# One early constant block instead of two layers' worth, group statistics in three groups, and the convolutional layers in a new order

## The chip, the core and the metric

The kernel runs on one NeuronCore of a Trainium2 chip. Such a core has five engines that run side by side: TensorE (PE) does matrix products and writes them to PSUM banks, VectorE (DVE) does elementwise work and reductions, ScalarE (ACT) does activations and copies, GpSimd (POOL) does elementwise work on SBUF, and SyncE (SP) issues transfers. Each engine works through its own list of instructions in order, and an instruction waits where it needs a semaphore that another engine, or a transfer, raises. The metric is the device time of one execution in microseconds (us), taken as the median of several runs.

## The reference, cut to what matters

The input is `x`, four images of 128 channels and 16 x 16 pixels. It goes through two convolutional layers (the first is an attention over the pixels of each image), then two attention layers with a small network each, on 256 tokens per image. The change touches the first two.

```python
def L0(x):                                  # attention over the pixels
    h = group_norm(x, gamma, beta)          # 32 groups of 4 channels, eps 1e-6
    q, k, v = (conv1x1(h, w, b) for w, b in ((wq, bq), (wk, bk), (wv, bv)))
    a = softmax(q.T @ k / sqrt(C))          # 256 x 256 for each image
    return x + conv1x1(v @ a.T, wp, bp)
def L1(x):                                  # squeeze and expand
    h = normalize_groups(x)                 # eps 1e-5
    s = relu(conv1x1(h, squeeze_w, squeeze_b))
    return x + concat(relu(conv1x1(s, expand1x1)), relu(conv3x3(s, expand3x3)))
# then: sliding-window attention, quantized linear layer, causal attention,
# and a mixture of 8 experts (2 per token), each behind a layer norm
```

## The kernel before, in words

Everything is in SBUF for the whole run. An image n (0 to 3) is one tile of 128 channels x 256 pixels: `xs` is the input, `hn` the normed image, `x1` the sum after the first layer (the trace writes `x`), `conv_out` the second layer's product, `t` the tokens (pixels on the partitions), `ht` the normed tokens and `hT` these turned back. `bank` are the 8 PSUM banks; an image has two of them in the convolutional layers (`two`), and an image of a pair has four of its own in the attention layers (`lane`). Images 0 and 1 are the pair that goes through the attention layer first, images 2 and 3 follow half a layer behind.

The order of the work is written out by hand: each engine's block is a long list of calls such as `first_project(1)` or `largest(0, 1, 2)`, one list for an engine, and only semaphores tie the lists together. No scheduler is at work.

The constants are one packed matrix of 4160 columns, `pk`. ACT loads the first 136 columns (`group`, `vecs`), SP loads the columns from `FIRST` to `EARLY` (semaphore `consts_in`) and from `EARLY` to the end (`consts2_in`), then the experts' weights.

Stages, with the names that the steps below use:

- Group statistics. DVE takes mean and variance of each channel (`first_stats`, `group_moments`), PE averages them over the four channels of a group with a product with `group` (`group_stats`), DVE makes a variance (`group_variance`), POOL raises it to -1/2 (L417, `grstd`), and DVE applies it (`affine` and `normed_input` in the first layer, `normed_residual` in the second). It is done for two pairs of images, `PAIRS`.
- First layer: `fold` multiplies wv by wp once, `first_project` makes q and k, `first_values` the values, `first_scores` the scores, DVE their maxima (`first_largest`) and ACT the exponentials (`first_exps`), DVE divides (`first_probs`), PE turns them (`first_turn`) and mixes the values (`first_mix`), DVE adds the input (`first_residual`, L1595).
- Second layer: `squeeze`, ACT and DVE copy it into a padded image (`squeezed`), `convolve`, ACT `convolved`, DVE `second_residual` (L1624).
- Tokens: `turn_tokens` on PE, `tokens` on DVE, `norm_variance` on DVE, POOL `power` (L381), DVE `norm` (L1437), PE `turn`, ACT `turned`.
- Entry of attention: PE `project_keys` (L889) and `project_queries` (L900), ACT `upper_keys` and `upper_queries`, DVE `lower_keys` (L1445) and `lower_queries` (L1451), PE `values`, DVE `copy_values`, `masked_keys` on DVE, ACT and POOL, PE `scores`, DVE `largest` (L1475), ACT `exps`, PE `turn_probs` (L955), and DVE or ACT copy them back.

`keep_clock` issues matmuls on a zeroed tile `idle_work` whose results nobody reads. POOL waits in `after_norm(0, 3)` for DVE's `norm(0, 3)`, then makes the quantized weight (L442 to L451) and splits the experts' weights into two parts (L432, L434), between which its parts of `masked_keys` and `power` for the next images stand.

Of the kernel before, what the change touches and what calls it, by code (L numbers as in the profile page):

```python
# [14 lines left out]
B, HH, WW = 4, 16, 16  # L15
# [34 lines left out]
EARLY = AT["aq"]  # L50
# [4 lines left out]
def build(nc, x, packed, w1, w2, routes, out):  # L55
    with ExitStack() as ctx:
# [312 lines left out]
        def _(pool):  # L369
# [43 lines left out]
            for j in range(2):  # L413
                for p, ns in enumerate(PAIRS):
                    pool.wait_ge(ve_ready, 2 * j + p + 1)
# [42 lines left out]
            power(0, 2)  # L458
            power(0, 3)
            masked_keys(0, 0)  # L460
# [74 lines left out]
        def _(act):  # L535
# [125 lines left out]
            first_exps(0)  # L661
            first_queries(2)
            first_keys(2)
            first_queries(3)
            first_keys(3)
            first_exps(1)
            first_exps(2)
            first_probs_turned(0)
# [4 lines left out]
            squeezed(0)  # L673
            squeezed(1)
            convolved(0)
            convolved(1)
            squeezed(2)
            squeezed(3)
            convolved(2)
            convolved(3)  # L680
            turned(0, 0)
            turned(0, 1)
            upper_keys(0, 0)
            upper_queries(0, 0)
# [3 lines left out]
            masked_keys(0, 1, 1)  # L688
            exps(0, 1, 0)
            exps(0, 0, 0)  # L690
# [87 lines left out]
            upper_keys(1, 2)  # L778
            masked_keys(1, 3, 0)
            upper_queries(1, 2)  # L780
            inverse_sums_turned(1, 1)
# [16 lines left out]
            exps(1, 2, 3)  # L798
            exps(1, 3, 4)
            exps(1, 2, 4)  # L800
            probs_turned(1, 3, 3)
            probs_turned(1, 2, 3)
            exps(1, 3, 5)
            exps(1, 2, 5)
            exp_of_gap(0)
            probs_turned(1, 3, 5)
            probs_turned(1, 2, 5)
            turn_routes(0)
            inverse_sums_turned(1, 3)
            inverse_sums_turned(1, 2)  # L810
# [30 lines left out]
        def _(pe):  # L841
            mm = nc.tensor.matmul

            def group_stats(j, p):
                pe.wait_ge(cs_ready, 2 * j + p + 1)
                ns = PAIRS[p]
                mm(two[ns[0]][1][:, 0:4], const("group"), cmv[:, ns[0]:ns[-1] + 1, :],
                   start=True, stop=True).then_inc(gs_ready, 1)
# [254 lines left out]
            def squeeze(n):  # L1103
                pe.wait_ge(hn_ready, B + n + 1)
# [873 lines left out]
```

## Time and profile before

| | us |
|---|---|
| median of 3 runs | 238.69 (238.41 to 238.84) |
| the profiled execution | 238.59 |
| its span, first to last instruction | 236.8 |
| PE busy | 225.3 |
| DVE busy | 204.7 |
| ACT busy | 168.1 |
| POOL busy | 92.1 |

The profiled execution is 1.79 us longer than its span, and 0.10 us shorter than the median. The two convolutional layers take the first 37 us, the two attention layers run to about 143 us, and the experts take the rest. The share of busy time does not say what bounds a stage; the waits in it do.

### The profile page before, as it was taken

What the parts mean: (1) busy time and instruction counts of PE and PEld (TensorE: products, weight loads), DVE (VectorE), ACT (ScalarE), POOL (GpSimd) and SP (SyncE); (2) the same over time, 40 slices, a digit from 0 to 9 for tenths busy, and PEclk for the clock granted to TensorE, in tenths of its full rate; (3) what the DMA queues carried; (4) which work ended last, traced back from release to release, by engine and by line L of the source; (5) the groups of instructions that cost most, each with busy time, mean ns of one, the idle gap of its engine ahead of it and who ended that gap; (6) DMA issues with size and microseconds to landing.
All of it is one profiled execution on the core that took longest, in us unless ns stands there. A gap on an engine that the chain in (4) does not pass through costs nothing.

```text
span 236.8 us, 4624 instructions
## 1 busy us (share of the span) xinstructions
PE 225.3 (95%) x1495; PEld 172.5 (73%) x1495; DVE 204.7 (86%) x524; ACT 168.1 (71%) x498; POOL 92.1 (39%) x155
## 2 busy tenths in 40 slices
PE   7899898999999999999999998999999999999995
PEld 2697566677776687676876675887888888888885
DVE  4678889985989989999798965999999996799986
ACT  2276355899769997799969968666557766666660
POOL 6200325668885856277825819924200000000000
PEclk9999999999999999999999999999999999999999
DMA  6910000000310300030000303510110002612001
GB/s 177 373 45 4 0 0 0 1 3 14 121 47 4 89 0 3 0 93 0 3 1 0 91 1 116 155 44 28 55 53 0 3 0 79 190 44 79 13 1 44
DMA packets 9463, 11.71 MB, mean 49 GB/s; under 512 B 720, under 2 KB 6096, under 8 KB 9312
## 3 DMA queue, kind: packets, MB, share of 16 engines
q1 hardware_dynamic: 9008, 11.16, 15.3%
q10 hardware_dynamic: 432, 0.27, 0.4%
q8 instruction: 12, 0.20, 0.3%
q14 instruction: 11, 0.09, 0.1%
HBM read 10.87 MB, written 0.56 MB: 48 GB/s over the span
## 4 chain that ended last, share of the span: by engine, by line
PE 61%; DVE 14%; ACT 9%; POOL 9%; DMA 3%; issue 3%; SPq 1%; POOLq 0%; ACTq 0%; DVEq 0%
PE bank L1031 6%; PE bank L1046 6%; PE bank L1043 6%; PE bank L1044 6%; PE bank L1033 6%; PE bank L1032 6%; ACT early_prob L588 4%; PE bank L955 4%; DVE negmax L1475 4%; POOL w_lo L434 3%; DMA pk<-packed 3%; PE bank L980 2%; PE bank L889 2%; PE bank L931 2%; POOL w_hi L432 2%
## 5 line engine op out<-in xcount | busy, mean ns | idle before, releaser
L821 ACT ACTIVATE hb<-bank,pk 128x512 f32<-128x512 f32 x64 | 43.0, 710 | 19.6 <-PE bank L1033 19.6
L1853 DVE TENSOR_TENSOR hlo<-hb,hhi 128x512 fp32r<-128x512 f32 x64 | 46.1, 741 | 4.8 <-ACT hhi L824 3.7
L588 ACT ACTIVATE prob<-bank,negmax 128x192 f32<-128x192 f32 (+1 forms) x64 | 28.8, 480 | 5.5 <-DVE negmax L1475 5.2
L1475 DVE TENSOR_REDUCE negmax<-bank 128x2 f32<-128x384 f32 (+2 forms) x48 | 29.8, 640 | 2.7 <-PE bank L937 2.3
L544 ACT ACTIVATE probT<-bank 128x512 f32<-128x512 f32 x38 | 23.0, 639 | 5.9 <-PE bank L955 4.3
L1031 PE MATMUL bank<-xhi,w_hi 128*128 128x512 f32 x64 | 25.6, 399 | 1.2 <-ACT hhi L824 1.1
L434 POOL TENSOR_TENSOR w_lo<-w_raw,w_hi 128x256 fp32r<-128x256 f32 x32 | 25.2, 788 | 2.6
L1043 PE MATMUL bank<-hhi,w_hi 128*128 128x512 f32 (+2 forms) x68 | 25.9, 381 | 0.0
L1046 PE MATMUL bank<-hlo,w_hi 128*128 128x512 f32 (+2 forms) x68 | 25.9, 381 | 0.0
L1044 PE MATMUL bank<-hhi,w_lo 128*128 128x512 f32 (+2 forms) x68 | 25.8, 380 | 0.0
L1033 PE MATMUL bank<-xhi,w_lo 128*128 128x512 f32 x64 | 25.0, 390 | 0.0
L1032 PE MATMUL bank<-xlo,w_hi 128*128 128x512 f32 x64 | 25.0, 390 | 0.0
L931 PE MATMUL bank<-kM,q_hi 128*128 128x512 f32 (+1 forms) x48 | 22.6, 471 | 1.6 <-ACT early_prob L588 1.0
L588 ACT ACTIVATE early_prob<-bank,negmax 128x128 f32<-128x128 f32 x64 | 23.3, 416 | 0.3 <-DVE negmax L1475 0.2
L824 ACT ACTIVATE hhi<-bank,pk 128x512 fp32r<-128x512 f32 x32 | 22.6, 707 | 0.0
L381 POOL TENSOR_TENSOR rstd<-ve,neghalf 128x2 f32<-128x2 f32 x16 | 11.6, 733 | 25.7 <-DVE ve L1432 25.7
L955 PE MATMUL bank<-pk,prob 128*128 128x128 f32 x128 | 19.4, 276 | 0.6 <-ACT prob L588 0.6
L432 POOL CAST w_hi<-w_raw 128x256 fp32r<-128x256 f32 x32 | 14.5, 453 | 11.2 <-DVE comb L1510 5.3
L409 POOL TENSOR_SCALAR kM<-k_parts,pk 128x256 fp32r<-128x256 f32 x32 | 17.4, 569 | 2.4 <-DVE k_parts L1445 2.3
L931 PE MATMUL bank<-kM,q_lo 128*128 128x512 f32 (+1 forms) x48 | 18.1, 376 | 0.0
L955 PEld LDWEIGHTS bank<-pk,prob 128*128 128x128 f32 x128 | 14.8, 141 | 3.2 <-issue 1.2
L588 ACT ACTIVATION_READ_ACCUMULATOR early_prob<-bank,negmax 128x1 f32 x64 | 16.4, 256 | 0.0
(159 smaller groups left out, 525.2 us busy)
## 6 DMA issues: line engine op xcount, KB each, us to landing
w_raw<-w SPq DMA_DIRECT2D x16, 256.0 KB, 3.1
comb_b<-routes SPq DMA_DIRECT2D x16, 256.0 KB, 3.2
pk<-packed SPq DMA_DIRECT2D x1, 1280.0 KB, 8.9
pk<-packed SPq DMA_DIRECT2D x1, 560.0 KB, 6.3
xs<-x SPq DMA_DIRECT2D x3, 128.0 KB, 2.6
out<-acc SPq DMA_DIRECT2D x3, 128.0 KB, 1.7
xs<-x ACTq DMA_DIRECT2D x1, 128.0 KB, 3.0
pk<-packed ACTq DMA_DIRECT2D x1, 68.0 KB, 2.5
```

Source lines behind the costliest of these rows:

```text
L588: last = nc.scalar.activation(prob_of(n, u)[:, of], lane[n][u % 2][:, of], ACT.Exp, bias=negmax[n][:, unit_query(u), h:h + 1], accum_out=s ...
L821: nc.scalar.activation(hb[blk % 2][:, j, :], h_bank[j][:, :], ACT.Relu, bias=bias).then_inc(h_ready, 1)
L931: mm(dst[:, :, keys], part[n % 2][:, g, i * 128:(i + 1) * 128], kM[n % 2][:, heads[0]:heads[-1] + 1, keys], start=(part is q_hi), stop=Fal ...
L955: last = nc.tensor.transpose(lane[n][2][:, i * 128:(i + 1) * 128], prob_of(n, u)[:, i * 128:(i + 1) * 128], ident)
L1031: mm(h_bank[j][:, :], w_hi[e][:, 0, chunk], xhi[:, cols], start=True, stop=False)
L1032: mm(h_bank[j][:, :], w_hi[e][:, 0, chunk], xlo[:, cols], start=False, stop=False)
L1033: mm(h_bank[j][:, :], w_lo[e][:, 0, chunk], xhi[:, cols], start=False, stop=True).then_inc(h_full, 1)
L1043: mm(sums, w_hi[e][:, 1, chunk], hhi[blk % 2][:, j, cols], start=(j == 0), stop=False)
L1044: mm(sums, w_lo[e][:, 1, chunk], hhi[blk % 2][:, j, cols], start=False, stop=False)
L1046: last = mm(sums, w_hi[e][:, 1, chunk], hlo[blk % 2][:, j, cols], start=False, stop=(j == HC - 1))
L1475: V.tensor_reduce(negmax[n][:, unit_query(u), heads[0]:heads[-1] + 1], lane[n][u % 2][:, :].rearrange("q (h k) -> q h k", h=len(heads))[:, ...
L1853: V.tensor_tensor(hlo[blk % 2][:, j, :], hb[blk % 2][:, j, :], hhi[blk % 2][:, j, :].bitcast(F32), ALU.subtract).then_inc(hlo_ready, 1)
```

## The change

Four things are changed. The early constant block ends before `squeeze` instead of before `aq` (640 columns instead of 1120), SP issues the third image behind it, and waits for it to land before it issues the other constants; `squeeze(0)` waits for these. Group statistics are made for images 0, 1 and the pair (2, 3) instead of two pairs, in both layers. The fixed lists of PE, DVE, ACT and POOL are written in a new order, mostly in the convolutional layers and at the entry of attention, with a few neighbours exchanged further on. The idle matmuls go from 8, 5, 1, 6 and 1 in a row to 8, 3, 3, 3, 1 and 1.

```diff
-EARLY = AT["aq"]
+EARLY = AT["squeeze"]
+GROUPS = (((0,), (1,), (2, 3)), ((0,), (1,), (2, 3)))
+def group_of(j, p):
+    return j * len(GROUPS[0]) + p
...
         def _(sp):
-            for n in range(B - 1):
+            for n in range(B - 2):
                 sp.dma_start(xs[n][:, :], x[n]).then_inc(x_in[n], 16)
             sp.dma_start(pk[:, FIRST:EARLY], packed[:, FIRST:EARLY]).then_inc(consts_in, 16)
+            sp.dma_start(xs[B - 2][:, :], x[B - 2]).then_inc(x_in[B - 2], 16)
+            sp.wait_ge(consts_in, 16)
             sp.dma_start(pk[:, EARLY:PACKED], packed[:, EARLY:PACKED]).then_inc(consts2_in, 16)
...
             def group_stats(j, p):
-                pe.wait_ge(cs_ready, 2 * j + p + 1)
-                ns = PAIRS[p]
-                mm(two[ns[0]][1][:, 0:4], const("group"), cmv[:, ns[0]:ns[-1] + 1, :],
+                pe.wait_ge(cs_ready, group_of(j, p) + 1)
+                if (j, p) == (1, 0):
+                    pe.wait_ge(w_mean_read, 1)
+                ns = GROUPS[j][p]
+                mm(two[ns[0]][j][:, 0:2 * len(ns)], const("group"), cmv[:, ns[0]:ns[-1] + 1, :],
...
             def first_values(n):
                 pe.wait_ge(fold_ready, 1)
+                pe.wait_ge(hn_ready, n + 1)
...
             def squeeze(n):
+                if n == 0:
+                    pe.wait_ge(consts2_in, 16)
...
             def group_moments(j, p):
-                ns = PAIRS[p]
+                ns = GROUPS[j][p]
...
             second_residual(2)
-            norm(0, 0)
+            norm(0, 1)
             second_residual(3)
-            norm(0, 1)
+            lower_queries(0, 0)
             tokens([2, 3])
-            norm_variance([2, 3])
+            norm_variance([2])
             lower_keys(0, 0)
-            lower_queries(0, 0)
             lower_keys(0, 1)
+            norm_variance([3])
```

The first instructions of DVE, from the first image's statistics to the variance of the first group; `cmv` holds each image's moments, `gve` the variance. Before:

```order
L1395 BN_STATS stats0<-xs0 128x6
L1395 BN_STATS stats1<-xs1 128x6
L1403 BN_AGGR cmv<-stats0 128x2
L1403 BN_AGGR cmv<-stats1 128x2
L1406 TENSOR_TENSOR csq<-cmv 128x2
L1407 TENSOR_TENSOR cmv<-cmv,csq 128x2
```

And in the changed kernel:

```order
L1414 BN_STATS stats0<-xs0 128x6
L1422 BN_AGGR cmv<-stats0 128x2
L1425 TENSOR_TENSOR csq<-cmv 128x1
L1426 TENSOR_TENSOR cmv<-cmv,csq 128x1
L1414 BN_STATS stats1<-xs1 128x6
L1422 BN_AGGR cmv<-stats1 128x2
```

The pair's steps on two columns have become one image's steps on one column, and the second image's own follow.

DVE again, where the second layer ends and attention begins: `x13` is image 3 after the second layer, `q_lo0` and `k_parts0` are the first lane's queries and keys. Before:

```order
L1624 TENSOR_TENSOR x13<-x13,conv_out3 128x256
L1437 TENSOR_SCALAR ht1<-t1,mv1,rstd1 128x128 x2
L1629 COPY t2<-bank3 128x256
L1629 COPY t3<-bank7 128x256
L1423 BN_STATS stats2<-t2 128x6 x2
L1423 BN_STATS stats3<-t3 128x6 x2
L1428 BN_AGGR mv2<-stats2 128x2 x2
L1428 BN_AGGR mv3<-stats3 128x2 x2
L1432 TENSOR_SCALAR ve2<-mv2 128x2
L1432 TENSOR_SCALAR ve3<-mv3 128x2
L1445 TENSOR_TENSOR k_parts0<-bank1,k_parts0 64x512
```

And in the changed kernel:

```order
L1456 TENSOR_SCALAR ht1<-t1,mv1,rstd1 128x128 x2
L1644 TENSOR_TENSOR x13<-x13,conv_out3 128x256
L1470 SCALAR_TENSOR_TENSOR q_lo0<-bank0,q_hi0 128x512
L1649 COPY t2<-bank3 128x256
L1649 COPY t3<-bank7 128x256
L1442 BN_STATS stats2<-t2 128x6 x2
L1447 BN_AGGR mv2<-stats2 128x2 x2
L1451 TENSOR_SCALAR ve2<-mv2 128x2
L1464 TENSOR_TENSOR k_parts0<-bank1,k_parts0 64x512
L1464 TENSOR_TENSOR k_parts1<-bank5,k_parts1 64x512
L1442 BN_STATS stats3<-t3 128x6 x2
```

`ht1` now stands ahead of `x13`, and `q_lo0`, which stood behind all of these rows, now follows `x13` directly.

PE at the same place, where `x13` is turned into tokens (bank7) and the first lane's projections follow. Before:

```order
L1099 MATMUL bank3<-pk,x12 128x128 x2
L862 MATMUL bank0<-pk,ht0 128x128 x2
L1099 MATMUL bank7<-pk,x13 128x128 x2
L862 MATMUL bank4<-pk,ht1 128x128 x2
L889 MATMUL bank1<-hT0,pk 128x256 x2
```

And in the changed kernel:

```order
L875 MATMUL bank0<-pk,ht0 128x128 x2
L1127 MATMUL bank2<-spad2,pk 128x256 x3
L1127 MATMUL bank6<-spad3,pk 128x256 x3
L1113 MATMUL bank3<-pk,x12 128x128 x2
L875 MATMUL bank4<-pk,ht1 128x128 x2
L1113 MATMUL bank7<-pk,x13 128x128 x2
L913 MATMUL bank0<-hT0,pk 128x256 x2
L902 MATMUL bank1<-hT0,pk 128x256 x2
```

The first lane's `ht0` is turned before the last two convolutions, the turn of `x13` is now the last matmul ahead of the projections, and the queries (L913) come before the keys (L902).

## Rows read from the trace of the kernel before

**Rows 1.** Windows: start:end, length, busy us (count) per engine, granted clock, DMA share, GB/s

```profile
core 0: us, PE busy (x) PEld busy (x) DVE busy (x) ACT busy (x) POOL busy (x), PEclk, DMA share, GB/s
0.00:12.00 12.00, 9.55 (x38) 5.49 (x39) 6.59 (x32) 3.42 (x8) 5.10 (x15) 1.00 0.82 276
...
28.00:37.00 9.00, 7.82 (x38) 5.71 (x36) 7.21 (x27) 4.57 (x11) 3.30 (x7) 1.00 0.00 0
37.00:50.00 13.00, 12.35 (x78) 8.88 (x77) 12.59 (x34) 10.19 (x40) 6.71 (x12) 1.00 0.00 1
50.00:66.00 16.00, 16.00 (x166) 12.44 (x165) 12.10 (x23) 14.55 (x54) 14.28 (x25) 1.00 0.19 61
```

**Rows 2.** Transfers of the page: count, KB each, median us from issue to landing

```profile
pk<-packed SPq DMA_DIRECT2D x1, 1280.0 KB, 8.9
pk<-packed SPq DMA_DIRECT2D x1, 560.0 KB, 6.3
```

**Rows 3.** Timeline, 0 to 12 us: start, us, engine, line, operation [idle before, releaser]

```profile
1.17 3.60 PE L1053 MATMUL bank<-idle_work 128*128 128x512 bf16 x8 [1.17 <-DVE idle_work L1633]
...
5.43 1.33 PE L1053 MATMUL bank<-idle_work 128*128 128x512 bf16 x5
...
6.39 0.70 POOL L417 TENSOR_TENSOR grstd<-gve,neghalf 128x2 f32<-128x2 f32 x1 [2.26 <-DVE gve L1415]
...
8.04 0.73 DVE L1573 TENSOR_SCALAR hn<-xs,ga,gb 128x256 f32<-128x256 f32 x2
...
8.41 0.49 PE L1093 MATMUL bank<-pk 128*128 128x128 f32 x2 [0.95 <-DMA pk<-packed]
...
8.88 0.68 PE L1057 MATMUL bank<-hn,pk 128*128 128x256 f32 x2
```

**Rows 4.** Windows of DVE alone: start:end, length, busy us (count), granted clock, DMA

```profile
11.78:36.52 24.74, 20.42 (x71) 1.00 0.04 13
19.98:28.26 8.28, 7.63 (x30) 1.00 0.01 2
36.52:49.14 12.62, 12.21 (x34) 1.00 0.00 1
```

**Rows 5.** DVE groups by line, 0 to 37 us: busy us, mean ns, idle before

```profile
L1573 DVE TENSOR_SCALAR hn<-xs,ga,gb 128x256 f32<-128x256 f32 x4 | 1.5, 406 | 0.0
L1406 DVE TENSOR_TENSOR csq<-cmv 128x2 f32<-128x2 f32 x4 | 0.6, 161 | 0.1
L1565 DVE TENSOR_TENSOR ga<-grstd,pk 128x1 f32<-128x1 f32 x4 | 0.5, 156 | 0.6 <-POOL grstd L417 0.6
```

**Rows 6.** Waits of DVE, 11.7 to 36.5 us: total us, times, longest

```profile
DVE negmax L1582 <- PE bank L1070: 1.7, 2, 1.3
DVE hn L1600 <- POOL grstd L417: 0.8, 1, 0.8
DVE rinv L1587 <- ACT prob L626: 0.7, 1, 0.7
DVE ht L1437 <- POOL rstd L381: 0.6, 1, 0.6
```

**Rows 7.** Timeline, 36 to 39.3 us, of DVE, then PE, then ACT

```profile
36.10 0.42 DVE L1624 TENSOR_TENSOR x<-x,conv_out 128x256 f32<-128x256 f32 x1
36.43 0.60 DVE L1437 TENSOR_SCALAR ht<-t,mv,rstd 128x128 f32<-128x128 f32 x2
36.95 0.75 DVE L1629 COPY t<-bank 128x256 f32<-128x256 f32 x2
...
39.19 0.69 DVE L1445 TENSOR_TENSOR k_parts<-bank,k_parts 64x512 fp32r<-64x512 f32 x1
...
36.57 0.44 PE L1099 MATMUL bank<-pk,x 128*128 128x128 f32 x2
...
37.36 1.03 PE L889 MATMUL bank<-hT,pk 128*128 128x256 f32 x4
...
38.43 0.60 ACT L544 ACTIVATE k_parts<-bank 128x512 fp32r<-128x512 f32 x1 [0.48 <-PE bank L889]
```

**Rows 8.** Timeline, 48.5 to 71 us, of DVE and POOL around POOL's long row of work

```profile
48.54 0.59 DVE L1437 TENSOR_SCALAR ht<-t,mv,rstd 128x128 f32<-128x128 f32 x2
...
49.23 0.73 POOL L442 TENSOR_SCALAR w_less<-pk,w_mean 128x128 f32<-128x128 f32 x1 [4.18 <-DVE ht L1437]
...
68.83 0.18 DVE L1432 TENSOR_SCALAR ve<-mv 128x2 f32<-128x2 f32 x1
...
69.79 0.73 POOL L381 TENSOR_TENSOR rstd<-ve,neghalf 128x2 f32<-128x2 f32 x1
...
70.56 0.60 DVE L1437 TENSOR_SCALAR ht<-t,mv,rstd 128x128 f32<-128x128 f32 x2 [0.50 <-POOL rstd L381]
```

More of the change, by code:

```diff
@@ L1174, in _ @@
             values(0, 1)
+            scores(0, 0, 0)
             scores(0, 1, 0)
-            scores(0, 0, 0)
             scores(0, 1, 1)
+            turn_probs(0, 0, 0)
             scores(0, 0, 1)
+            scores(0, 0, 2)
             turn_probs(0, 1, 0)
             scores(0, 1, 2)
-            turn_probs(0, 0, 0)
-            scores(0, 0, 2)
+            turn(0, 2)
             scores(0, 1, 3)
-            turn(0, 2)
             mix(0, PAIRS[0], 0)
@@ L1221, in _ @@
             turn_probs(0, 3, 0)
+            scores(0, 2, 2)
+            turn_probs(0, 2, 0)
             scores(0, 3, 2)
-            turn_probs(0, 2, 0)
-            scores(0, 2, 2)
             turn(1, 1)
@@ L1645, in _ @@
+            affine(1)
+            group_moments(0, 2)
             normed_input(1)
-            affine(1)
+            first_values(0)
+            group_variance(0, 2, 1e-6)
+            affine(2)
+            first_largest(0)
             normed_input(2)
             normed_input(3)
-            first_values(0)
-            first_largest(0)
+            first_largest(1)
+            first_probs(0)
             weight_sums()
-            first_probs(0)
-            first_largest(1)
+            first_probs(1)
@@ L1677, in _ @@
-            squeezed(0)
+            group_moments(1, 2)
+            second_residual(0)
             squeezed(1)
-            group_variance(1, 1, 1e-5)
+            group_variance(1, 2, 1e-5)
+            tokens([0])
+            norm_variance([0])
             normed_residual(2)
             normed_residual(3)
-            second_residual(0)
+            second_residual(1)
+            norm(0, 0)
             squeezed(2)
-            second_residual(1)
+            tokens([1])
             squeezed(3)
-            tokens([0, 1])
@@ L1698, in _ @@
             lower_queries(0, 1)
-            masked_keys(0, 0, 0)
+            largest(0, 0, 0)
             copy_values(0, 1)
+            masked_keys(0, 0, 1)
             largest(0, 1, 0)
-            masked_keys(0, 0, 1)
-            largest(0, 0, 0)
             largest(0, 1, 1)
+            copy_probs(0, 0, 0)
             largest(0, 0, 1)
+            norm(0, 2)
             copy_probs(0, 1, 0)
-            norm(0, 2)
-            copy_probs(0, 0, 0)
+            norm(0, 3)
             largest(0, 0, 2)
-            norm(0, 3)
@@ L1825, in _ @@
             norm(3, 0)
+            largest(1, 3, 3)
+            logits(1)
             largest(1, 2, 3)
-            logits(1)
-            largest(1, 3, 3)
             largest(1, 3, 4)
```

150 lines of the change are left out of this document (78 added, 72 removed).

## The prediction

> **What bounds the kernel now.** I read first the windows by stage [rows 1], then the transfers and the first 12 us [rows 2, 3], then DVE's windows, groups and waits in the convolutional layers [rows 4 to 6], and last the hand-over to attention [rows 7, 8]. The reader should see three things. First, from 37 us on there is hardly a hole to fill: PE is busy 12.35 of 13 us and then 16.00 of 16, and DVE 12.59 of the first 13 [rows 1]. What stands behind 37 us is hardly changed in amount, so a gain must be made in the first 37 us and be handed over whole. Second, in the first 12 us the transfers fill the DMA engines to 0.82, and the early constants take 6.3 us to land [rows 1, 2]: `fold` starts at 8.41, released by them, and the first projection only behind it at 8.88, though its normed image was ready at about 8.4 (half of the pair's 0.73 us from 8.04) [rows 3]. Third, from 11.78 to 36.52 DVE is busy 20.42 of 24.74 us [rows 4], and its waits there are on single partners (1.7 + 0.8 + 0.7 + 0.6 us) [rows 6]. The new order is aimed at these 4.3 us.
>
> How tight can DVE be packed? From 19.98 to 28.26 it shows no wait worth a row and is busy 7.63 of 8.28 us, 92%; the rest is the hand-over between small dependent instructions [rows 4]. At the entry of attention, where the instructions are longer, it is 12.21 of 12.62, 97% [rows 4].
>
> **The constants.** The early block falls from 560 to 320 KB, has one image less ahead of it, and nothing queued beside it. In the first 12 us the core moved 276 KB per us on the mean [rows 1], so the 240 + 128 KB that are gone ahead of its landing, and the 1280 KB no longer mixed with it, bring it to about 5 us. It is then no longer the late one. Next late is the first normed image: PE's 8 idle matmuls last until 4.77 [rows 3], so the first group product starts at about 4.8 instead of at 5.0 although image 0's moments are ready at 4.1; DVE's three small steps, POOL's 0.70 us [rows 3], then the second group's variance, `affine(0)` and `first_stats(0, 2)`, which now stand before `normed_input(0)`, put it at about 8.15. First projection 8.25 instead of 8.88: 0.6 us gained. It does not last. `normed_input(1)` has `first_stats(0, 3)`, `affine(1)` and the pair's moments ahead of it (0.4 + 0.35 + 0.7 us), comes at 9.9 instead of 8.8, and the second projection starts at about 10.0 instead of 10.27. The other 1520 KB are issued at about 5.3 and land, at 276 to 360 KB per us, between 11.3 and 14.5 with the experts' weights beside them (1280 KB took 8.9 us under such company [rows 2]). `weight_sums` on DVE, the first that needs them, comes at about 15.3; `squeeze(0)` near 24. Cost nothing; if they were late DVE would stall, see the rivals.
>
> **Group statistics in three groups.** Each layer gets one more group. That is five more DVE instructions (two in the moments, three in the variance) of 0.16 us each [rows 5], with gaps 0.19 us: 0.95 us of DVE for a layer. Halving the width saves nothing: a 128x1 instruction took 156 ns, a 128x2 one 161 [rows 5]. One POOL step more a layer, 0.70 us, is off the path for the groups that are early.
>
> The Trainium skill (VectorE: DVE Perf Modes, section "The TRN2 errata") says that a large tile pays a fixed latency once and many small tiles pay it each; it speaks against this edit, and by its table's 58 cycles at 0.96 GHz, an estimate, the five would be about 0.3 us a layer. The two rows side by side agree with the rule and not with that size.
>
> **The convolutional layers.** Because `normed_input(2)` and `(3)` have moved behind the third group's variance, POOL's step, `affine(2)` and `first_largest(0)`, DVE has more left to do at 11.78, where it takes up `affine(2)` (I placed it by adding up POOL's step behind the variance at 10.9). Work to the end of `second_residual(3)`, which I call R3: the 20.42 us that the old kernel does in the same stretch [rows 4], plus `affine(2)` 0.54, two normed images 0.73 [rows 3, 5], one more group 0.80, and `norm(0, 1)`, which now stands before R3, 0.60 [rows 7]: 23.1 us. At 92% to 95% that is 24.3 to 25.1 us, so R3 falls at 36.1 to 36.9 with no wait on anyone. Following the lists by hand I find 0.5 to 0.9 us of waits left (for conv_out of images 2 and 3 and for POOL's `power(0, 1)`). R3 is at 36.6 to 37.8, I take 37.2, against 36.52 [rows 7]: **+0.7 us**. Below, packing without any gap would give 34.9, 1.6 us less. The holes were found, but the moved and added work fills them. The images 0 and 1 are ahead (`ht0` ready near 33, not 36.2), images 2 and 3 are behind, and the hand-over needs all four, because PE's turn of `x13` stands before the first projection.
>
> **The entry of attention.** In the old order R3 is followed on DVE by `norm(0, 1)`, two copies and both `norm_variance`, all of which hide the way PE, ACT need to the first keys: DVE takes `k_parts0` at 39.19, 2.7 us after R3, without rest [rows 7]. In the new one `lower_queries(0, 0)` follows R3 directly. It needs PE's turn of `x13` (0.05 + 0.22 us after R3, as 36.57 follows 36.52), then the queries' projection, from whose start to ACT's start it is 1.07 us (37.36 to 38.43), and ACT's 0.60 us [rows 7]: 0.3 + 1.07 + 0.60 = **2.0 us in which DVE has nothing it may do**. Queued behind the waiting instruction are the tokens of images 2 and 3, `norm_variance([2])` and both `lower_keys`; for these wait PE's values and scores and ACT's masked keys. What is given back: `norm(0, 1)` is already done (0.60) and one `largest` (0.55) now follows `norm(0, 3)` instead of leading it. So from R3 to the end of `norm(0, 3)`: (12.21 - 0.60 - 0.55) / 0.97 = 11.4, + 2.0, + 0.15 for the split variance = 13.6 us against 12.6 [rows 4]: +1.0 us. That end releases POOL at 49.23, and POOL then works without a hole to `power(1, 1)` at 69.79, whose input had been there since 69.0; DVE waits for it [rows 8]. So POOL's path is +1.0 us and DVE, PE's path, a `largest` further back, about +1.5. I take +1.2 for both, with bounds of 0.7 (the slack of 0.8 us at 69 us spares a part) and 2.0 (nothing is given back). The rest (some 20 exchanged neighbours, as many instructions as before) I put at 0, bounds -0.3 and +0.3.
>
> **Sum.** 238.59 (the profiled execution) + 0.7 + 1.2 = 240.5 us; the median is 0.10 above that execution, inside the rounding. The bounds are 238.59 - 1.6 + 0.7 - 0.3 = 237.4 and 238.59 + 1.3 + 2.0 + 0.3 = 242.2.
>
> **Rivals.** *Faster (0.20).* The mechanism is the packing of DVE before 36 us: if the small instructions overlap better than 92% and no wait is left, R3 comes at 34.9 to 35.3, 1.2 to 1.6 us earlier, and of the entry only 0.7 to 1.0 is lost: 237.4 to 238.1. A start of the stretch before 11.78 works the same way. It decides at R3 = 35.3. For it: 4.3 idle us in the old stretch [rows 4]; against it: 2.7 us of work more in it. *No change (0.12).* R3 at about 35.6 or so with the entry's stall partly absorbed by PE's 0.65 us of rest between 37 and 50 us [rows 1]: 238.2 to 239.1. This is also the case in which the change only shifts holes. *Late constants (0.04).* If the 1520 KB land at 16.5, DVE stands 1.2 us in `weight_sums` with the first layer's divisions behind it: 241.7. *The clock falls (0.06).* The old kernel is granted 1.00 in every window [rows 1], the upper level of 2.4 GHz, and PE never rests long; in the new entry PE would be idle for most of 3.5 us, between the second lane's projection and the first score, with only two short value products in it. Idle matmuls took 3.60 us for 8 at the start and 1.33 us for 5 after it [rows 3], so work at the slow level costs about 0.2 us more for every 0.2 us: three us of it add 1.5 to the sum, 242.0.
>
> The Trainium skill (TensorE: Matmul & The Clock Gate, section "Part 1: The HAM clock gate") holds that rest brings the array's clock to 1.2 GHz, half rate; by that rule the last rival could occur, and no granted clock below 1.00 in the trace of before shows it.
>
> **How the numbers follow.** The forecast 240.5 has 0.58. Slower by over 0.2% (0.5 us, about what a measurement of this kernel can tell from no change) is the forecast with late constants and falling clock, 0.68; within it 0.12; faster 0.20. The range must leave out at most 0.2: from 238.2, which leaves out most of the faster case, to 242.4, which takes in the bound of the sum and the clock.
>
> **What would show it.** In the new profile: `fold` released by PE's own order and not by a transfer, first projection near 8.2; second projection near 10.0; DVE over 90% busy from 12 to 36 us; R3 at 36.6 to 37.8; a wait of about 2 us of DVE's `q_lo` on ACT's `q_hi` right behind R3, where the old kernel has 0; POOL's L442 row 1.7 to 2.5 us later than 49.23; the experts starting later by as much and lasting as long. I am wrong if R3 is before 36, or if the stall is there and POOL's row still starts at 49. I am also wrong if the experts' stage takes another length, which no step here touches.

## The result, and the profile after

The changed kernel takes **241.25 us** (median of 14 executions, 239.18 to 242.29) against 238.46 us (14 executions, 238.12 to 238.86) for the kernel before: ratio 1.0107, 95% interval 1.0083 to 1.0130. It is slower, by 2.8 us. A second measurement on another chip gave 240.8 against 238.97 us, ratio 1.0085, 1.0049 to 1.0121. The time goes with TensorE's mean granted clock (1.0 is the upper level of 2.4 GHz throughout): the 14 executions had 1.0 once (239.45 us), 0.997 once (239.18), 0.993 five times (240.3 to 240.95), and 0.983 to 0.986 seven times (241.56 to 242.29). The profiled execution took 242.11 us, with a span of 240.2 and a clock of 0.986.

The page after: span, granted clock in 40 slices of 6 us, and the two constant transfers, to set beside [rows 2]:

```profile
span 240.2 us, 4645 instructions
...
PEclk9999999679999999999999999999999999999999
...
pk<-packed SPq DMA_DIRECT2D x1, 1520.0 KB, 6.5
...
pk<-packed SPq DMA_DIRECT2D x1, 320.0 KB, 4.2
```

Two slices, from 42 to 54 us, stand at 6 and 7 tenths. The windows after, with the columns of [rows 1], then DVE alone in the convolutional layers, as in [rows 4]:

```profile
28.00:37.00 9.00, 7.65 (x36) 5.29 (x37) 7.81 (x28) 4.75 (x11) 3.09 (x7) 1.00 0.00 0
...
37.00:50.00 13.00, 10.37 (x41) 7.26 (x40) 9.47 (x24) 6.64 (x20) 5.48 (x10) 0.77 0.00 1
...
50.00:66.00 16.00, 16.00 (x148) 11.96 (x148) 12.16 (x24) 14.63 (x64) 11.39 (x21) 0.97 0.11 34
```

```profile
11.43:36.79 25.36, 22.88 (x83) 1.00 0.13 43
```

Between 37 and 50 us PE is busy 2 us less than before, DVE 3.1 us less, and the clock is down. Waits after (total us, times, longest), of DVE from 11.4 to 36.8 us, which answer [rows 6]:

```profile
DVE ga L1584 <- POOL grstd L428: 0.8, 1, 0.8
DVE x L1614 <- PE bank L1102: 0.6, 1, 0.6
DVE x L1644 <- ACT conv_out L664: 0.2, 1, 0.2
...
11.43 0.23 DVE L1584 TENSOR_TENSOR ga<-grstd,pk 128x1 f32<-128x1 f32 x2 [0.81 <-POOL grstd L428]
```

The first of these waits ends at 11.43, as its timeline row shows, so it lies ahead of the window of DVE from 11.43 to 36.79. Inside that window DVE waits 0.9 us.

The start after, which answers [rows 3] (timeline: start, us, engine, line, operation):

```profile
1.17 3.60 PE L1066 MATMUL bank<-idle_work 128*128 128x512 bf16 x8 [1.17 <-DVE idle_work L1653]
...
4.85 1.44 PE L1066 MATMUL bank<-idle_work 128*128 128x512 bf16 x3
...
7.11 0.38 PE L1107 MATMUL bank<-pk 128*128 128x128 f32 x2
...
7.67 0.40 DVE L1592 TENSOR_SCALAR hn<-xs,ga,gb 128x256 f32<-128x256 f32 x1
...
8.12 0.70 PE L1070 MATMUL bank<-hn,pk 128*128 128x256 f32 x2
...
9.68 0.68 PE L1070 MATMUL bank<-hn,pk 128*128 128x256 f32 x2
...
14.45 0.28 DVE L1625 TENSOR_REDUCE w_sum<-pk 128x1 f32<-128x128 f32 x1
```

`fold` (L1107) waits for no transfer, and `weight_sums` (L1625) finds its constants there. The hand-over to attention after, which answers [rows 7, 8]:

```profile
36.36 0.43 DVE L1644 TENSOR_TENSOR x<-x,conv_out 128x256 f32<-128x256 f32 x1
...
38.19 0.60 ACT L555 ACTIVATE q_hi<-bank 128x512 fp32r<-128x512 f32 x1 [1.05 <-PE bank L913]
38.81 0.69 DVE L1470 SCALAR_TENSOR_TENSOR q_lo<-bank,q_hi 128x512 fp32r<-128x512 f32 x1 [2.03 <-ACT q_hi L555]
...
42.02 1.32 PE L921 MATMUL bank<-pk,hT 128*128 128x128 f32 x8 [1.29 <-DVE k_parts L1464]
...
44.61 0.66 PE L944 MATMUL bank<-kM,q_hi 128*128 128x384 f32 x1 [1.27 <-DVE kM L1480]
...
53.26 0.73 POOL L453 TENSOR_SCALAR w_less<-pk,w_mean 128x128 f32<-128x128 f32 x1 [6.40 <-DVE ht L1456]
```

R3 is the end of the last row of `x<-x,conv_out`, 36.79. DVE stands 2.03 us behind it, and PE then has two holes of 1.3 us with 1.3 us of value products between them.

**Four pieces.** Four marks can be read in every profile: the start of the first projection (first row of PE with `hn,pk`), R3, the start of POOL's `w_less` (L442 before, L453 after), and the end of the span. The table gives the start of the first projection, the lengths between the marks and the span in us, for the profiled execution of each kernel; the experiments' kernels are described below.

| kernel | first projection | to R3 | R3 to `w_less` | `w_less` to end | span |
|---|---|---|---|---|---|
| before | 8.88 | 27.64 | 12.71 | 187.6 | 236.8 |
| after | 8.12 | 28.67 | 16.47 | 186.9 | 240.2 |
| after, on the other chip | 7.59 | 28.66 | 15.66 | 187.0 | 238.9 |
| a_keep | 7.63 | 28.68 | 14.25 | 186.9 | 237.5 |
| b_entry | 7.50 | 28.71 | 12.70 | 186.9 | 235.8 |
| b_both | 7.32 | 28.67 | 12.76 | 187.0 | 235.7 |
| k_both (the same kernel) | 8.15 | 28.65 | 12.74 | 186.9 | 236.4 |
| g_masked | 8.29 | 28.57 | 12.74 | 186.9 | 236.5 |
| h_start | 7.36 | 28.70 | 12.75 | 186.9 | 235.7 |
| f_small_new | 7.52 | 29.39 | 12.74 | 186.9 | 236.5 |
| i_const_old | 9.93 | 29.86 | 12.74 | 186.9 | 239.4 |
| c_before_q | 9.36 | 27.64 | 16.30 | 187.5 | 240.8 |
| d_const | 9.23 | 28.06 | 12.71 | 187.6 | 237.6 |
| e_small | 10.02 | 29.19 | 12.73 | 187.5 | 239.4 |

The pieces are almost independent of each other: each changes where an edit touches it, and what the first projection gains or loses is handed to R3 whole. The exceptions are d_const, e_small and i_const_old, whose first projections also ran slowly (see the last section). Before to after it is -0.8, +1.0, +3.8 and -0.6 us. The first two nearly cancel, and the third piece holds more than the whole loss.

### The profile page after: what moved, and what is told of

Read it like the earlier page. It is cut to its first block, busy times and chain, and to the rows that moved or that the text cites. A ratio compares the mean times of both kernels' runs of the same rounds, so it can differ in the third digit from the quotient of the medians.

```text
span 240.2 us, 4645 instructions
## 1 busy us (share of the span) xinstructions
PE 228.3 (95%) x1496; PEld 174.6 (73%) x1497; DVE 205.8 (86%) x534; ACT 168.6 (70%) x498; POOL 90.3 (38%) x157
## 4 chain that ended last, share of the span: by engine, by line
PE 63%; DVE 16%; POOL 9%; ACT 8%; issue 3%; ACTq 0%; POOLq 0%; DVEq 0%
PE bank L1044 6%; PE bank L1056 6%; PE bank L1059 6%; PE bank L1057 6%; PE bank L1045 6%; PE bank L1046 6%; PE bank L968 4%; ACT early_prob L599 3%; PE bank L944 3%; POOL w_lo L445 3%; PE bank L1066 3%; DVE negmax L1494 3%; PE bank L993 2%; POOL w_hi L443 2%; ACT probT L555 2%
## 5 line engine op out<-in xcount | busy, mean ns | idle before, releaser
L1881 DVE TENSOR_TENSOR hlo<-hb,hhi 128x512 fp32r<-128x512 f32 x64 | 44.3, 714 | 7.4 <-ACT hhi L835 6.3
L944 PE MATMUL bank<-kM,q_hi 128*128 128x512 f32 (+1 forms) x48 | 24.0, 501 | 2.5 <-DVE kM L1480 1.3
L445 POOL TENSOR_TENSOR w_lo<-w_raw,w_hi 128x256 fp32r<-128x256 f32 x32 | 24.3, 759 | 2.6
L968 PE MATMUL bank<-pk,prob 128*128 128x128 f32 x128 | 19.9, 281 | 0.8 <-ACT prob L599 0.8
L944 PE MATMUL bank<-kM,q_lo 128*128 128x512 f32 (+1 forms) x48 | 18.9, 394 | 0.0
L968 PEld LDWEIGHTS bank<-pk,prob 128*128 128x128 f32 x128 | 15.3, 144 | 3.5 <-issue 1.4
L420 POOL TENSOR_SCALAR kM<-k_parts,pk 128x256 fp32r<-128x256 f32 x32 | 16.5, 536 | 2.3 <-DVE k_parts L1464 2.1
L950 PE MATMUL bank<-pk 128*128 128x384 bf16 (+2 forms) x48 | 17.1, 356 | 0.0
```

The lines of the kernel that those rows point to most:

```text
L944: mm(dst[:, :, keys], part[n % 2][:, g, i * 128:(i + 1) * 128], kM[n % 2][:, heads[0]:heads[-1] + 1, keys], start=(part is q_hi), stop=Fal ...
L968: last = nc.tensor.transpose(lane[n][2][:, i * 128:(i + 1) * 128], prob_of(n, u)[:, i * 128:(i + 1) * 128], ident)
L1881: V.tensor_tensor(hlo[blk % 2][:, j, :], hb[blk % 2][:, j, :], hhi[blk % 2][:, j, :].bitcast(F32), ALU.subtract).then_inc(hlo_ready, 1)
```

## Experiments

**Is it the stall, or the clock behind it?** Three kernels part the two. In a_keep the stall stays and idle matmuls fill PE's holes:

```
             project_queries(0, 1)
+            keep_clock(lane[0][2][:, :], 6)
             values(0, 0)
             values(0, 1)
+            keep_clock(lane[0][2][:, :], 5)
```

> The changed kernel with 6 idle matmuls on PE behind the second lane's projections and 5 behind the value products, in the two holes of 1.3 us each that its trace shows at 40.7 and 43.3 us. Nothing else moves. Theory 1 (stall and clock): DVE's 2.0 us stall leaves PE these holes, the granted clock falls to 0.51 for 6.5 us behind them, and that costs up to 2.7 us on top of the stall. Filled, the clock stays at 1.00, every execution takes 239.2 to 239.6 us, as the two executions at 0.997 and 1.00 did, and the scatter of 3 us is gone. Theory 2 (waits only): the time is lost in waits and in the added DVE work, and the low clock lies in their shadow; then the median stays at 241.0 to 241.5.

Measured: 239.3 us (239.11 to 239.9), clock 0.998 or more in every execution, ratio to before 1.0011 (0.9986 to 1.0036). The windows, with the columns of [rows 1], first of after, then of a_keep:

```profile
37.00:44.00 7.00, 5.06 (x26) 4.01 (x25) 4.88 (x16) 3.92 (x9) 2.62 (x6) 1.00 0.00 1
44.00:50.50 6.50, 5.81 (x17) 3.58 (x17) 4.82 (x9) 3.23 (x16) 2.85 (x5) 0.51 0.00 0
```

```profile
37.00:44.00 7.00, 6.89 (x34) 4.56 (x33) 5.36 (x16) 4.10 (x8) 3.10 (x6) 1.00 0.00 1
44.00:50.50 6.50, 6.08 (x33) 3.73 (x34) 6.46 (x15) 4.44 (x24) 2.82 (x5) 1.00 0.01 3
```

and a_keep's wait of DVE in the same stretch:

```profile
DVE q_lo L1472 <- ACT q_hi L555: 2.0, 1, 2.0
```

The work that computes is the same and the stall is the same 2.0 us; only PE's holes are filled. The granted clock stays at 1.00 where it had been 0.51 (nearly all of the window at the lower level, 1.2 GHz), and 1.95 us come back (241.25 to 239.3). The two medians are of separate measurements; by the ratios to the kernel before beside each, 1.0107 and 1.0011, it is 2.3 us. The changed kernel's own executions say the same: 239.2 and 239.45 us at a clock of 0.997 or more, against 241.92 at the median of the seven lowest clocks. So the fallen clock costs 2.0 to 2.3 us of a loss of 2.8.

In b_entry the stall goes, and nothing is done for the clock:

```
             second_residual(3)
-            lower_queries(0, 0)
             tokens([2, 3])
             norm_variance([2])
+            lower_queries(0, 0)
             lower_keys(0, 0)
```

> The changed kernel with lower_queries(0, 0) moved on DVE behind the copies of tokens 2 and 3 and norm_variance([2]), two calls further down, all else as it is. Theory 1: the 2.03 us wait on ACT's q_hi is filled by 1.8 us of work that is there anyway; keys come 1.6 to 1.8 us earlier, PE's holes shrink from 1.3 and 1.3 us to under 1.0 in sum, the clock stays at 1.00, and the time is 237.9 to 238.8 us, level with the kernel before. Theory 2 (the convolutional layers carry the loss, more DVE work): the second residual of image 3 ends only 0.3 us later than before, so little is left for it; if it were the cause the time would stay above 240.

Measured: 237.91 us (237.57 to 239.63), ratio 0.9972 (0.9941 to 1.0004). Eight of 12 executions had a clock of 0.997 or more and took 237.6 to 238.2 us; four had 0.993 and took 239.4 to 239.6. b_entry's window and rows:

```profile
37.00:44.00 7.00, 5.64 (x29) 4.32 (x27) 6.35 (x19) 4.10 (x9) 4.69 (x9) 1.00 0.00 1
```

```profile
38.24 0.69 DVE L1470 SCALAR_TENSOR_TENSOR q_lo<-bank,q_hi 128x512 fp32r<-128x512 f32 x1
...
48.91 0.73 POOL L453 TENSOR_SCALAR w_less<-pk,w_mean 128x128 f32<-128x128 f32 x1 [3.75 <-DVE ht L1456]
```

`q_lo` waits for nothing now, and `w_less` starts 4.35 us earlier than in after. One PE hole of 1.1 us in front of the scores is left, and the clock still fell in a third of the executions. The profiled one kept it, so no trace shows where it fell; that it was behind this hole is argued from b_both, where the hole is filled. b_both is b_entry with four idle matmuls at each of the two places of a_keep:

> The changed kernel with the moved lower_queries of b_entry and 4 + 4 idle matmuls in the same two places as a_keep. Theory 1: the same 237.9 to 238.8 us as with the move alone, since nothing is left for the idle matmuls to guard; if the move alone still shows a low clock in some executions, this one shows none. Against a_keep it should be 1.0 us faster, which is the price of the stall at full clock.

Measured: 237.95 us (237.45 to 238.47), clock 0.997 or more in every execution, ratio 0.9956 (0.9931 to 0.9981). Its window:

```profile
44.00:50.50 6.50, 6.36 (x50) 4.21 (x50) 6.21 (x15) 5.97 (x31) 2.65 (x5) 1.00 0.01 3
```

At full clock the stall is worth 239.3 - 237.95 = 1.35 us (in the profiles 14.25 - 12.76 = 1.5). The same kernel, measured again as k_both in a later set of four kernels on another chip:

> The changed kernel with the mended entry and 4 + 4 idle matmuls (the same as b_both), beside the changed kernel itself. Theory 1: 237.7 to 238.2 us with clocks of 0.997 or more, 3 us under the changed kernel and 0.3 to 0.6% under the kernel before; the gain is that of the new order in the convolutional layers and of norm(0, 1) done ahead of the hand-over.

gave 237.9 us (237.52 to 238.4), ratio 0.9933 (0.9895 to 0.9971). It was 2.9 us under the changed kernel on the same chip (j_after, next). **It beats both kernels**, by 0.4% and 0.7% over the kernel before in the two measurements: what is left of the change is a small gain once the one instruction group stands two entries further back and the holes are filled. With the move alone (b_entry) the interval still reaches 1.0004. The 0.7% is helped by ten executions of the kernel before at 241 us; against the median of its other 25, 238.71, it is 0.3%.

That set, the last one, also held the changed kernel once more, so that all four share a chip:

> The changed kernel as it is, once more, on the same chip as the next three. Theory 1: 240 to 242.3 us, falling into levels by the mean granted clock: about 239.3 at 1.00, 240.5 at 0.993, 242 at 0.986. Theory 2: no such order between time and clock.

Measured: 240.8 us (239.4 to 242.18). Its profiled execution had a clock of 0.993, and its window says the same as after's in smaller size. The median is 1.4 us above its one execution at 0.997 (239.4).

```profile
37.00:44.00 7.00, 4.52 (x23) 3.51 (x21) 5.39 (x17) 4.10 (x8) 3.16 (x6) 1.00 0.01 1
44.00:50.50 6.50, 6.14 (x24) 3.91 (x25) 5.27 (x11) 3.60 (x18) 2.77 (x5) 0.74 0.00 0
```

**The same edit in the old order.** c_before_q moves `lower_queries(0, 0)` in the kernel before, and nothing else:

```
             norm(0, 1)
+            lower_queries(0, 0)
             tokens([2, 3])
             norm_variance([2, 3])
             lower_keys(0, 0)
-            lower_queries(0, 0)
```

> The kernel before with one DVE call moved: lower_queries(0, 0) directly behind norm(0, 1), ahead of the copies of tokens 2 and 3 and both norm_variance. PE still projects keys first, so q_hi is there only at 39.9: DVE stands 2.8 us. Theory 1: the stall alone makes the kernel slower, by 1.5 to 2.5 us at full clock, and with a fallen clock by up to 5: 240.2 to 243.5 us, with granted clocks below 1.00 in the records. Theory 2: the stall is absorbed and the time stays within 0.5 us of 238.5.

Measured: 242.85 us (242.36 to 244.28), ratio 1.0167 (1.0116 to 1.0218). Its windows:

```profile
37.00:44.00 7.00, 4.39 (x23) 3.34 (x21) 3.98 (x17) 3.15 (x6) 0.84 (x2) 1.00 0.00 0
44.00:50.50 6.50, 6.28 (x27) 4.37 (x28) 5.77 (x11) 3.85 (x15) 5.11 (x9) 0.74 0.00 1
```

The stall on DVE, and PE's hole behind it:

```profile
40.40 0.69 DVE L1451 SCALAR_TENSOR_TENSOR q_lo<-bank,q_hi 128x512 fp32r<-128x512 f32 x1 [2.89 <-ACT q_hi L544]
...
44.00 1.73 PE L908 MATMUL bank<-pk,hT 128*128 128x128 f32 x8 [2.54 <-DVE k_parts L1445]
```

One moved line makes the old kernel 3.9 us slower, with a stall of 2.89 us (here PE projects the keys first, so the queries come later) and a fall of the clock (0.74), and the third piece grows from 12.71 to 16.30 while the stretch before R3 keeps its 27.64. So a loss of this kind needs nothing else of the change. Its first projection at 9.36 instead of 8.88 is not the edit's, which stands 28 us later; see the last section.

**The constants.** d_const is the kernel before with that part alone: early block of 320 KB, third image behind it, the wait on SyncE, and `squeeze(0)` waiting for the second block.

```
-EARLY = AT["aq"]
+EARLY = AT["squeeze"]
...
-            for n in range(B - 1):
+            for n in range(B - 2):
...
+            sp.dma_start(xs[B - 2][:, :], x[B - 2]).then_inc(x_in[B - 2], 16)
+            sp.wait_ge(consts_in, 16)
```

> The kernel before with the constants' part of the change alone: early block of 640 columns, third image behind it, SP's wait, and the wait of squeeze(0). Groups and order as before. Theory 1: fold is released about 3 us earlier, the first projection starts at 8.5 instead of 8.88, and the 0.4 us are lost again within the first layer because DVE waits there on PE and ACT in turn: 0 to 0.4 us faster, 238.1 to 238.6 against a kernel before of 238.5. Theory 2 (the constants are what the new kernel with a mended entry gains): 0.5 to 1.0 us faster.

Measured: 239.36 us (238.64 to 241.85), ratio 1.0031 (1.0009 to 1.0052): slower, against what I expected. Its rows show why:

```profile
5.76 0.76 DVE L1399 BATCH_NORM_STATS2 stats<-xs 128x6 f32<-128x256 f32 x2 [0.68 <-DMA xs<-x]
6.43 0.14 DVE L1417 COPY gmv<-bank 128x4 f32<-128x4 f32 x1
...
8.40 0.64 PE L1095 MATMUL bank<-pk 128*128 128x128 f32 x2
...
9.23 1.02 PE L1059 MATMUL bank<-hn,pk 128*128 128x256 f32 x2
```

`fold` waits for no transfer any more. But the third image, now behind the early block, comes late, and in the old order DVE takes its statistics before the first pair's variance; the variance, which starts with the copy to `gmv`, is at 6.43 instead of 5.68. The earlier constants are paid for with a later image that DVE's queue wants first. This is not all of it: the first projection starts 0.35 us later than before and takes 1.02 us for 0.68, because PE was still slow (its five idle matmuls took 2.29 us for 1.33), and the second projection is 0.7 us late (10.97 for 10.27). So about half of the delay in this profile is the late image, and half the slow PE. Whether the earlier constants have a part in the slow PE is open.

i_const_old asks the reverse question: b_both with the old constants, so that only this part is missing.

> The same as k_both with the constants as they were before the change: early block of 1120 columns, the third image ahead of it, no wait on SP. Theory 1: the first projection waits again for the constants until about 8.9 us instead of starting at 7.3 to 8.1, and since DVE is full from 11.4 us on, the delay is paid whole: 0.8 to 1.2 us slower than k_both, 238.6 to 239.2. Theory 2 (the constants are hidden anyway): as k_both within 0.3 us.

Measured: 239.79 us (239.25 to 241.73), ratio 1.0037 (0.9997 to 1.0076), 1.9 us above k_both on the same chip and more than I had expected. Its rows:

```profile
8.51 0.49 PE L1105 MATMUL bank<-pk 128*128 128x128 f32 x2 [1.57 <-DMA pk<-packed]
...
9.93 1.06 PE L1068 MATMUL bank<-hn,pk 128*128 128x256 f32 x2
...
12.73 0.42 DVE L1597 COPY v<-bank 128x256 f32<-128x256 f32 x1 [3.38 <-PE bank L1075]
...
PEclk9799999999999999999999999999999999999998
```

In the new order `fold` is waited for by PE, and then by DVE for 3.4 us, because its copy of the first values stands ahead of the normed images 2 and 3. The 3.4 us are not the order's alone. Five of the 12 executions had a clock of 0.990 to 0.993 and 241.1 to 241.7 us, the profiled one (241.24) among them, and its second slice shows where: behind PE's hole of 1.57 us the granted clock is 0.82 from 8 to 10 us, 0.50 from 10 to 12 and 0.82 from 12 to 14, and the first projection takes 1.06 us for 0.7. The other seven took 239.25 to 239.79, at the median 1.7 us over k_both; its first projection is 1.8 us later than k_both's (9.93 for 8.15), which is that much. So the constants' part costs 0.6 to 0.7 us in the old order and brings 1.7 to 1.9 us in the new one, the fallen clock of five executions included: the two parts belong together, and a part that is taken alone can point the wrong way.

**The small instructions.** e_small adds five 128x2 products into a spare tile behind `group_variance(0, 1)` and five behind `group_variance(1, 1)` of the kernel before; f_small_new adds the same to b_both, behind `group_variance(0, 2)` and `(1, 2)`.

```
+            def spend(times):
+                for _ in range(times):
+                    step(V.tensor_tensor(spare[:, :], gsq[:, 0:2], gsq[:, 0:2], ALU.mult))
```

> The kernel before with five more small dependent DVE instructions (128x2 products into a spare tile) behind the second pair's variance in each layer, ten in all, 0.16 us each with gaps of 0.03. It is the work of one more group a layer without its use. Theory 1: the old order has 4.3 us of idle DVE before 36.5 us, but the first five stand directly ahead of the first normed image and the last five in the packed stretch from 20 to 28 us, so most is paid: 1.0 to 1.9 us slower. Theory 2 (added small work is hidden by the old waits): within 0.4 us of the kernel before.

> The changed kernel with the mended entry and idle matmuls (b_both) and the same five small DVE instructions behind the third group's variance in each layer. Theory 1 (DVE is full from 11.4 to 36 us in the new order): the second five are paid in full, 0.95 us, the first five stand ahead of a wait of 0.8 us for POOL and are hidden: 0.9 to 1.2 us slower than b_both, 238.9 to 239.2. Theory 2 (waits on the other engines decide in the new order too): under 0.5 us.

Measured: e_small 241.18 us (239.3 to 242.44; nine executions), ratio 1.0082 (1.0052 to 1.0113), in two levels: four executions at 239.3 to 239.9, five at 241.2 to 242.4. f_small_new 238.61 us (238.29 to 238.94), ratio 0.9994 (0.9971 to 1.0017), which is 0.0038 or about 0.9 us over b_both's ratio, 0.7 us by the medians; over g_masked, which was measured beside it and differs from b_both by an exchange without effect, it is 0.5 us. Its R3 piece is 29.39 against 28.67 us. Ten small instructions of 0.16 us, 1.9 us with their gaps, cost 0.5 to 0.9 us in the new order. The first five stand in the place of DVE's wait of 0.8 us for POOL, which is gone from that trace; of the other five, 0.95 us, 0.7 is found at R3. In the old order the median puts the ten at 2.0 to 2.4 us, but this is mostly something else: the profile, of the upper level, has PE still slow at 12 us, and its first projection and the products behind it take 1.22, 1.06 and 1.06 us where they took 0.68, 0.59 and 0.61 before, 1.5 us in all. The four executions of the lower level, 239.43 at the median, are 0.7 us over the kernel before (238.75), so, if that level is the undisturbed one, the instructions cost about as much in the old order as in the new.

**Two attempts to go further.** g_masked takes b_both's masked keys ahead of `norm_variance([3])`:

```
             lower_keys(0, 1)
+            masked_keys(0, 0, 0)
             norm_variance([3])
-            masked_keys(0, 0, 0)
```

> b_both with masked_keys(0, 0, 0) moved on DVE ahead of norm_variance([3]). PE waits 1.1 us for these masked keys in the mended entry. Theory 1: the first scores start 0.85 us earlier, but DVE has the same work until norm(0, 3), which releases POOL's long row, so the gain is small: 0 to 0.4 us, 237.5 to 238.0. Theory 2 (the first scores set the pace, not DVE's sum): 0.8 us faster, about 237.1.

Measured: 238.08 us (237.5 to 238.35), ratio 0.9972 (0.9961 to 0.9983). No gain over b_both; the piece from R3 to `w_less` is 12.74 in both. PE's first score starts at 43.07 against 43.09 in k_both: the masked keys were not held up by the variance, so the exchange frees nobody. DVE's work up to `norm(0, 3)` is the same in sum, which would keep the piece as it was; this is argued, not shown.

h_start takes one idle matmul from the first group of b_both and two from the next:

```
-            keep_clock(rest_a, 8)
+            keep_clock(rest_a, 7)
             pe.wait_ge(group_in, 16)
             group_stats(0, 0)
-            keep_clock(rest_a, 3)
+            keep_clock(rest_a, 1)
```

> The same as k_both with 7 idle matmuls instead of 8 ahead of the first group's product and 1 instead of 3 ahead of the second's. In the traces these stand in PE's queue ahead of the group products, and take 0.43 us each until PE is fast. Theory 1: both products come earlier, by up to 0.4 and 0.9 us, the first normed image by about 0.4, and it is paid out whole: 237.3 to 237.7. Theory 2: with fewer idle matmuls PE becomes fast later, the fold and the first projection run at half rate and the time rises by 0.3 to 1.0 us, or scatters more.

Measured: 237.62 us (237.51 to 239.71), ratio 0.9957 (0.9917 to 0.9998). Eight executions took 237.51 to 237.65, closest together of this study, though the lowest of b_both (237.45) and k_both (237.52) are no higher; the other four 239.37 to 239.71, all at a granted clock of 1.0. The profiled one's first projection (7.36) is no earlier than b_both's (7.32), so the edit does not beat a good start, and the ratio is no better than k_both's 0.9933. Both theories were partly right. What lengthens those four can't be read, since none of them is the profiled one; it stays open.

## Why the prediction was right, and where it was not

241.25 us lies in the range of 238.2 to 242.4, 0.75 above the forecast of 240.5, and the direction, slower, had the greatest chance. The stall was where it was said to be, in the size that was said. But the sum of 1.9 us came near the 2.8 us partly by luck: a fallen clock that the forecast left out costs 2 us, and gains that it did not see give back more than 1 us. By its steps, with the four pieces:

- **Constants: read rightly in the main.** The first projection came at 8.12 us for 8.25, the second at 9.68 for 10.0, the early block landed in 4.2 us, `weight_sums` waited for nothing. Two things were missing. Nobody asked what the start is worth if it is passed on: what the first projection gains is found again at R3 to within 0.15 us, in the eight profiles whose order is the same up to R3 (28.57 to 28.71). And the start scatters: 7.32 to 8.29 us with the same edit, so the profile of after (8.12) is at the late end. "It does not last" was right of the second projection and wrong of the rest: the missing part cost 1.7 to 1.9 us in i_const_old.
- **Group statistics: count and price held.** DVE was busy 22.88 us to R3, forecast 23.1. Of the two layers' 1.9 us the sum for R3 held only one group, 0.80, and f_small_new's R3 piece grew by 0.72; the first layer's group fell into a wait. The Trainium skill (VectorE: DVE Perf Modes, section "The TRN2 errata") says that many small tiles each pay a fixed latency; f_small_new agrees in direction, 0.5 to 0.9 us for ten of them.
- **Convolutional layers: the stretch right, its start too late.** From `affine(2)` to R3 37.2 - 11.78 = 25.4 us were forecast and 25.36 measured, with 0.9 us of waits for 0.5 to 0.9 by hand, and 93% busy outside them (22.88 of 24.5) for 92% to 95%. But the stretch began at 11.43. From first projection to R3 it grew by 1.0 us (27.64 to 28.67) where 37.2 - 8.25 - 27.64 = 1.3 was forecast. With the earlier start that gives R3 at 36.79 in after and 35.99 to 36.86 in the kernels that share its order up to there, not at 37.2. The wait for conv_out was 0.2 us; the longer one, 0.6 for PE's product ahead of the first residual, was not among those named. The term of +0.7 measured +0.3 in after and -0.5 in b_both. I had written that I am wrong if R3 is before 36; at full pace it is at 36.
- **Entry of attention: the mechanism right, the give-back wrong.** The stall was 2.03 us for 2.0. Of it 1.0 was to come back, because `norm(0, 1)` and one `largest` had left the stretch. It did not. Without the stall the new order needs 12.70 us from R3 to `w_less`, as the old one does (12.71), where the same working gives 11.6 to the end of `norm(0, 3)`, 0.1 us ahead of `w_less`: DVE's busy time there fell by 0.3 us only (11.87 in b_both, 12.21 before), as the copies of the tokens and the split variance took longer, and its share from 97% to 94%, with two waits of 0.17 us on ACT. So at full clock the stall costs 1.5 us at `w_less` and 1.35 at the end, for a forecast of 1.2: inside the bounds, for another reason. `w_less` was to start 1.7 to 2.5 us later than 49.23; it started 4.0 later, and 1.3 later at full clock (a_keep, 50.56), so this sign was missed on both sides.
- **What follows 50 us: not 0 but -0.6.** `w_less` to the end is 187.5 to 187.6 us in all four profiles of the old order and 186.9 to 187.0 in all ten of the new one. The bound of -0.3 was too narrow. Parted at POOL's `power` row near 100 us and at PE's first product with `hhi` near 150, where the experts are at work, it is +0.5 (49.3 to 49.9), -0.6 (50.1 to 49.45) and -0.5 us (88.1 to 87.55). The last is a sign of the prediction that went against it: the experts' stage was to keep its length. Which exchanged neighbours bring the three was not tried, so their cause stays open.
- **The clock: this step failed.** It was a rival at 0.06, with 3 us of slow work and 1.5 us. It came in 12 of 14 executions and cost 1.95 us at the median, for 6.5 us of slow work in the profiled one. The argument had all its parts: PE mostly idle, two short value products, the price of slow work from [rows 3]. What failed was the chance, since "every window of before shows 1.00" said nothing of a PE with holes, and the change made holes. It is not quite the stall's alone either: of 31 executions of the kernel before beside the first experiments two had a mean clock of 0.985 and 0.986 (241.99 and 242.1 us), and so had one of 12 of d_const (0.986); no profile shows where in them. That rest brings the clock to 1.2 GHz, half rate, stands in the Trainium skill (TensorE: Matmul & The Clock Gate, section "Part 1: The HAM clock gate"); the trace agrees with the level (0.51 over 6.5 us), but here PE had not rested at a stretch: it had been busy 5.06 of the 7 us before, with holes of 1.3 us.

Put together: forecast +0.7 and +1.2 and 0; measured at the median -1.0 for everything but stall and clock (b_both against before beside it, its filling matmuls included), +1.35 for the stall, +1.95 for the clock. These sum to 2.3 of 2.8 us; the rest is that before was 238.92 beside the first experiments and 238.46 beside after. By ratios it is 1.0107 = 1 + 0.0096 (clock) + 0.0055 (stall) - 0.0044. So the no-change and faster rivals were nearer than they looked: with one line moved and the holes filled the change is a gain of 0.4% to 0.7%. (The faster rival's own figures, -1.2 to -1.6 and +0.7 to +1.0, add up to 237.7 to 238.4 and not to 237.4 to 238.1.)

## What to carry to other kernels

When an instruction group that ends a chain over several engines (turn, projection, copy) is placed directly behind the group that starts the chain, add up the chain: on an engine that works in order it is a stall of just that length. Then look at what PE does in that time, for holes on PE can cost more than the stall through the clock (here 1.95 against 1.35 us), and a few idle matmuls in them cost 0.3 us at most (237.66 us for b_entry's eight executions that kept the clock, 237.95 for b_both). Mark the same three or four events in every profile and compare the pieces between them; that parts the causes, and shows which gains are really handed on.

## What the runs showed of the hardware

**The clock fell though PE never rested for long.** In after it went from 1.00 to 0.51 behind two holes of 1.3 us, with PE busy 5.06 of the 7 us before; with those holes filled (a_keep, b_both, k_both) it stayed, in 36 executions of 36. In i_const_old it went to 0.50 from 10 to 12 us, behind one hole of 1.57 us. The same program could go either way: b_entry kept the clock in eight of 12 executions. The steps of the mean clock, 0.993 and 0.986, go with about +1.3 and +2.6 us in after, but 0.993 goes with +1.9 in b_entry. At the lower level a score product of 128x512 that starts at 47.57 took 0.63 us, one at 52.74, back at full rate, 0.40:

```profile
47.57 0.63 PE L944 MATMUL bank<-kM,q_lo 128*128 128x512 f32 x1
...
52.74 0.40 PE L944 MATMUL bank<-kM,q_lo 128*128 128x512 f32 x1
```

**PE's pace at the start scatters, and the column of the granted clock doesn't show it.** Over the first 12 us it reads 1.00 [rows 1], yet the idle matmuls of 128x512 take 0.43 us each at first and 0.22 later. When they become quick differs from one execution to the next. The first rows of PE in b_both:

```profile
1.17 3.35 PE L1066 MATMUL bank<-idle_work 128*128 128x512 bf16 x8 [1.17 <-DVE idle_work L1655]
4.50 0.81 PE L1066 MATMUL bank<-idle_work 128*128 128x512 bf16 x3
```

and in e_small, where five stand in the second group:

```profile
5.54 2.29 PE L1054 MATMUL bank<-idle_work 128*128 128x512 bf16 x5
...
10.02 1.22 PE L1058 MATMUL bank<-hn,pk 128*128 128x256 f32 x2 [0.88 <-DVE hn L1578]
```

The first group of three took 0.81 us (b_both), 0.87 (b_entry), 1.05 (a_keep) and 1.44 (after), with the first projection at 7.32, 7.50, 7.63 and 8.12; the five of the old order 1.33 [rows 3], 2.12 in c_before_q and 2.29 in e_small. These matmuls stand ahead of a small product that the whole start waits for, and the delay reaches the end. That explains 0.8 us of the scatter between executions of one kernel (b_both and k_both, 237.58 and 238.32 us profiled). It can reach further: in e_small PE was slow, or slow again, past 12 us, 1.5 us more, with 1.00 in the column and 0.998 as the mean clock. Ten of 35 executions of before beside the last set took 240.97 to 241.57 us at that same mean clock, 0.998 to 0.999. They may be the same case, but none of them was profiled, and their cause stays open.
